# Attention, recurrence and experts on one core: the first stage split into two halves of the heads, all of it ahead of the tiles

## What is computed

```python
# 1. cross attention of every position to one target per element, 16 heads of 8
q = shard(query @ Wq + bq).reshape(b, H * s, hd)     # H = 16, s = 128, hd = 8
scores = softmax(einsum('bnd,bdh->bnh', q, k) / sqrt(hd))
context = einsum('bnh,bhd->bnd', scores, v)
context = context.transpose(0, 2, 1).reshape(b, s, H * hd)   # row of the result: d * 16 + h
# 2. linear attention: softmax of q over 8 values, elu(k) + 1, cumulative sums over the heads, @ Wo, + x
# 3. a gated recurrence over the 128 positions, then a top-2 of 8 experts FFN of its states, + x
```

## Time and profile before

| what | value |
|---|---|
| median of 3 runs | 395.06 us (394.81 to 395.1) |
| the profiled execution | 397.36 us, its span 395.7 us |
| PE busy | 369.5 us (93%) |
| VectorE busy | 336.7 us (85%) |
| ScalarE busy | 273.5 us (69%) |
| GpSimd busy | 264.3 us (67%) |
| mean granted TensorE clock | 0.939 |

### The profile page before, as it was taken

The page is one execution under the profiler, slowest core; times in us unless marked ns, Lnnn a source line. Parts: engine busy times, 40 slices in busy tenths (PEclk is TensorE's granted clock), DMA queues, the critical chain, the costliest instruction groups (busy, mean ns, idle before and its releaser), DMA issues.

```text
span 395.7 us, 9033 instructions
## 1 busy us (share of the span) xinstructions
PE 369.5 (93%) x2404; PEld 302.6 (76%) x2404; DVE 336.7 (85%) x1226; ACT 273.5 (69%) x1040; POOL 264.3 (67%) x293
## 2 busy tenths in 40 slices
PE   4999985578999999999999999999999999999995
PEld 2688851366788888888888888888888888878874
DVE  2677756876599999999999999999999999998640
ACT  2455545234488888888888887788788888877663
POOL 3977607883567777777777777777777777786000
PEclk9999995555599999999999999999999999999999
DMA  6600000000000000000000000000000000000000
GB/s 173 241 2 0 3 0 0 2 0 1 0 9 7 8 10 7 9 8 9 10 12 9 7 9 7 8 10 7 9 8 9 8 8 8 7 11 12 9 8 13
DMA packets 7584, 6.74 MB, mean 17 GB/s; under 512 B 880, under 2 KB 6256, under 8 KB 7536
## 3 DMA queue, kind: packets, MB, share of 16 engines
q1 hardware_dynamic: 7536, 6.19, 5.2%
HBM read 4.09 MB, written 2.10 MB: 16 GB/s over the span
## 4 chain that ended last, share of the span: by engine, by line
DVE 50%; issue 14%; PE 13%; ACT 1%; POOL 1%; DVEq 1%
DVE kvs L939 13%; PE bank L372 12%; DVE att L948 7%; DVE mem L997 5%; DVE h L1017 4%; DVE rden L931 4%; DVE bank L1002 3%; DVE bank L1009 3%; DVE kvs L917 3%; DVE bank L899 2%; PE bank L514 1%; DVE bank L923 1%; DVE bank L971 1%; POOL qc L329 1%; DVE res L988 1%
## 5 line engine op out<-in xcount | busy, mean ns | idle before, releaser
L329 POOL TENSOR_TENSOR qc<-kvs,qn 128x512 f32<-128x512 f32 x64 | 81.4, 1272 | 19.5 <-DVE kvs L939 15.2
L372 PEld LDWEIGHTS bank<-h,gwh 128*128 128x128 f32 x512 | 72.7, 201 | 20.8 <-DVE h L1017 17.9
L317 POOL TENSOR_TENSOR kv<-kv,qkv 128x512 f32<-128x512 f32 x64 | 81.0, 1268 | 3.3 <-DVE kvs L939 0.8
L939 DVE TENSOR_TENSOR_SCAN kvs<-bank,kv 128x256 f32<-128x256 f32 x128 | 81.4, 659 | 0.5 <-POOL qc L329 0.5
L372 PE MATMUL bank<-h,gwh 128*128 128x32 f32 x512 | 76.5, 274 | 4.7 <-DVE h L1017 4.6
L709 ACT ACTIVATE hid<-bank,gw 128x128 f32<-128x128 f32 x256 | 76.3, 372 | 1.6 <-PE bank L372 1.5
L372 PE MATMUL bank<-w,h 128*128 128x512 f32 x128 | 73.0, 653 | 0.0
L372 PE MATMUL bank<-w,hsq 128*128 128x128 f32 x512 | 71.2, 282 | 1.8 <-ACT hsq L717 1.8
L735 ACT ACTIVATE gt<-bank 128x64 f32<-128x64 f32 x128 | 30.2, 236 | 50.9 <-PE bank L372 49.9
L372 PEld LDWEIGHTS bank<-w,hsq 128*128 128x128 f32 x512 | 62.2, 191 | 3.4 <-ACT hsq L717 2.9
L372 PE MATMUL bank<-h,whw 128*128 128x64 f32 x256 | 52.6, 289 | 0.0
(11 more groups left out here) (112 smaller groups left out, 704.6 us busy)
## 6 DMA issues: line engine op xcount, KB each, us to landing
XT<-in_x_t_dram SPq DMA_DIRECT2D x8, 256.0 KB, 5.6
out_dram<-res SPq DMA_DIRECT2D x32, 64.0 KB
w<-in_w_dram SPq DMA_DIRECT2D x2, 512.0 KB, 5.1
aw<-in_aw_dram SPq DMA_DIRECT2D x1, 192.0 KB, 5.5
gwx<-in_gw_dram SPq DMA_DIRECT2D x1, 128.0 KB, 4.6
gwh<-in_gw_dram SPq DMA_DIRECT2D x1, 128.0 KB, 4.2
cwk<-in_cwk_dram SPq DMA_DIRECT2D x1, 64.0 KB, 1.9
cwv<-in_cwv_dram SPq DMA_DIRECT2D x1, 64.0 KB, 2.0
```

The costliest lines, as they stand in the source:

```text
L317: pool.tensor_tensor(kv[:, a * D:b * D, :].rearrange("p (d e) h -> p d e h", d=D // 2), kv[:, D * D + a:D * D + b, :].unsqueeze(2).broadca ...
L329: pool.tensor_tensor(qc[:, a:b, :, :], kvs[:, a * D:b * D, :].rearrange("p (d e) h -> p d e h", d=D // 2), qn[:, p, a:b, :].unsqueeze(2).b ...
L372: return pe.matmul(dst, w, rhs, start=start, stop=True, skip_group_check=True)
L939: dve.tensor_tensor_scan(flat(kvs[:, a:b, :]), scan_mask, flat(kv[:, a:b, :]), 0.0, ALU.mult, ALU.add).then_inc(kv_sum, 1)
```

## The change

Part 1 is still 16 units, but a unit is now four elements with eight heads. Units 0 to 7 are heads 0 to 7 of all 32 elements, units 8 to 15 heads 8 to 15. A unit's scores fill one bank as before, as four matmuls of 128 columns in place of two of 256; its context is the same four matmuls of 72 columns. All queries are kept (`qT` of 8 groups), and all keys (`kbd` of 32 elements), so GpSimd no longer waits for `s_ps` of an earlier unit. `q_of` for all groups now stands in the first eight units. The two matmuls for `awc` and `qkvb` move from units 12 and 14 to units 5 and 6. The three priming matmuls are gone, since Z, MEM and QKV are now scores banks themselves.

Units 8 to 15 have one bank (`OUT`) for their contexts. `context(u)` there waits for `normalise(u - 1)`, where before it waited for `normalise(u - 2)`.

The ramp of each engine begins with units 9 to 15, and the tiles' part of the ramp is rewritten: on VectorE `add_dims(0)` and `residual(0)` come directly behind `sum_heads(0, 3)`, and all of tile 1, then all of tile 2 come behind them. On PE `qkv_of(2)` and `(3)` go behind `gates_x(0, 0)`. The memsets and small copies that stood behind the last unit stand between units 6 and 7.

```diff
-PAIRS = B // 2
+QUADS = B // GROUP
+HALF = H // 2
...
-        qT = sb("qT", [P, 2, GROUP * P])
-        kbd = sb("kbd", [P, 4, H, H])
+        qT = sb("qT", [P, QUADS, GROUP * P])
+        kbd = sb("kbd", [P, B, H, H])
...
+        def scores_bank(u):
+            return Z if u % 2 else QKV if u < QUADS else MEM
+        def probs_bank(u):
+            return TR if u % 2 else MEM if u < QUADS else HID
+        def context_bank(u):
+            return OUT if u >= QUADS else ATT if u % 2 else DV
...
             def scores(u):
-                pe.wait_ge(q_sb, u // 2 + 1)
+                half, g = u // QUADS, u % QUADS
+                pe.wait_ge(q_sb, g + 1)
                 if u == 0:
-                    pe.wait_ge(kbd0_ok, 2)
-                else:
-                    pe.wait_ge(kbd_ok, 2 * u)
+                    pe.wait_ge(kbd0_ok, 1)
+                pe.wait_ge(kbd_ok, u + 1)
                 at_least(pe, s_sub, u - 1)
...
             def context(u):
                 pe.wait_ge(pT_sb, u + 1)
-                at_least(pe, c_sb, u - 1)
-                pe.wait_ge(vbd_ok, u + 1)
+                at_least(pe, c_sb, u if u >= QUADS else u - 1)
+                pe.wait_ge(vbd_ok, u % QUADS + 1)
...
-            for u in range(PAIRS):
-                if u + 1 < PAIRS:
-                    scores(u + 1)
-                if u % 2 == 0 and u // 2 + 1 < B // GROUP:
-                    q_of(u // 2 + 1)
+            q_of(1)
+            for u in range(QUADS):
+                scores(u + 1)
+                if u + 2 < QUADS:
+                    q_of(u + 2)
                 probs_T(u)
                 if u:
                     context(u - 1)
-                if u == PAIRS - 4:
+                if u == QUADS - 3:
                     pe.wait_ge(w_late, LATE_ALL)
-                    mm(bank[6][:, 0:3 * P], cwoT[:, :], aw[:, :]).then_inc(awc_ps, 1)
-                if u == PAIRS - 2:
+                    mm(HID[:, 0:3 * P], cwoT[:, :], aw[:, :]).then_inc(awc_ps, 1)
+                if u == QUADS - 2:
                     pe.wait_ge(awc_sb, 1)
-                    mm(bank[6][:, 0:3 * P], bco.broadcast_to([P, P]), aw[:, :]).then_inc(awc_ps, 1)
-            pe.wait_ge(s_sub, PAIRS - 1)
-            mm(Z[:, :], w1[:, 0, :], w1[:, 0:4, :].rearrange("p e d -> p (e d)")).then_inc(prime_z, 1)
-            pe.wait_ge(pT_sb, PAIRS - 1)
-            mm(MEM[:, :], w1[:, 0, :], w1[:, 0:4, :].rearrange("p e d -> p (e d)")).then_inc(prime_m, 1)
-            pe.wait_ge(c_sb, PAIRS - 1)
-            mm(QKV[:, :], w1[:, 0, :], w1[:, 0:4, :].rearrange("p e d -> p (e d)")).then_inc(prime_q, 1)
-            context(PAIRS - 1)
+                    mm(HID[:, 0:3 * P], bco.broadcast_to([P, P]), aw[:, :]).then_inc(awc_ps, 1)
+            context(QUADS - 1)
             pe.wait_ge(consts, 2)
-            pe.wait_ge(c_sb, PAIRS)
...
             def ramp():
+                scores(9)
+                probs_T(8)
...
                 qkv_of(0)
                 qkv_of(1)
-                qkv_of(2)
-                qkv_of(3)
                 att_T(0)
                 project_out(0)
                 gates_x(0, 0)
+                qkv_of(2)
+                qkv_of(3)
```

## The result

| | before | the change |
|---|---|---|
| median | 395.08 us (394.81 to 398.7, 4 runs) | 411.26 us (409.25 to 413.11, 4 runs) |
| ratio to before | | 1.0386, 95% interval 1.0307 to 1.0466 |
| profiled execution, its span | 397.36 us, 395.7 us | 413.11 us, 411.4 us |
| mean granted clock in it | 0.939 | 0.921 |

The change is slower by 16.2 us in the medians and by 15.7 us in the spans of the two profiled executions. The forecast was slower by 10.6, 405.6 with a range to 410.0. The direction and the largest term were right; the sum was too small by 5.7 us in the median and by 5.1 in the span.

What follows compares the result with a forecast made beforehand. PE limits the first stage, a VectorE, ScalarE and GpSimd chain the ramp. +3.0 us to `head_max(0)` and +6.8 in the ramp make +9.8; with +0.8 for the clock, 395.06 becomes 405.6 us, range 399.5 to 410.

Steps and rivals of the forecast that it cites:

- The tiles' order in the ramp, +6.8: Ramp, `head_max(0)` to `memory(0, 0, 0)`: tile 1, then tile 2 begin later, making 24.2 us against 17.4.
- PE's walk through the units, 38.7 from `scores(1)` to `context(11)`: First stage: walking the engines' lists from `scores(1)` near 13.9 us puts `context(11)` at 52.6.
- The single bank, 2.12 a context: Last contexts: the one bank spaces them, four times 2.12 us from `context(11)` at 52.6 to `context(15)` at 61.1.
- The clock in this chain: "I take +0.8": Late contexts: low clock likely falls before or at `qkv_of(0)`, +0.8 us, plus 0.85 per context behind the fall.
- +2.5 as the upper end: Late contexts: the most the low clock was taken to cost if it falls before several contexts, up to +2.5 us.
- The start: "`scores(1)` starts near 13.9": Start of PE: `scores(1)` waits for the late keys, near 12.4 us, and starts near 13.9, where it was 12.16.
- The clock in the tiles: unchanged: First three tiles: clock returns in the third tile again, so `memory(0, 0, 0)` to the fourth tile stays about 38 us.
- the likeliest case: Whole kernel: the forecast with the clock returning in the third tile again, 403.5 to 408 us, chance 0.56.
- The rival (one tile sooner): First tiles: the full clock is back one tile sooner, giving 399.5 to 402 us; chance 0.2.

Runs made afterwards that it cites:

- the old order: The changed kernel with tiles 0, 1 and 2 interleaved in the ramp as before on PE, ScalarE and VectorE: 404.08 us, ratio to before 1.0144.
- two banks: The changed kernel with contexts 8 to 15 alternating between banks ATT and OUT, each waiting for normalise(u - 2): 402.21 us, ratio to before 1.0117.
- The fillers: The changed kernel with one extra, never-read matmul of 512 or 384 columns in each gap between contexts 11 to 15: 405.55 us, ratio to before 1.0217.
- the one with the early matmuls: The changed kernel with nine small, never-read identity matmuls in PE's idle time before the first scores: 410.07 us, ratio to before 1.0295.
- two filled versions: The kernel before with never-read matmuls in PE's idle time of ramp and tile 0; the second adds more, also in tile 1: 394.04 and 393.33 us.

## Why the prediction was right and where it was wrong

- **The tiles' order in the ramp, +6.8.** Measured +6.94, and 17.40 with the old order. Every part of the chain came as worked out: tile 1 begins 11.9 behind the first `head_max`, tile 2 6.0 behind that, and GpSimd's `weigh(1)` ends it.
- **PE's walk through the units, 38.7 from `scores(1)` to `context(11)`.** Measured 38.86. The halved scores matmuls cost next to nothing, as taken (a unit with a projection 3.08 us, before 3.06). The match to 0.2 is in part luck: from `scores(1)` to the end of `context(7)` it was 25.6 against 24.9, and the second half won 0.5 of that back.
- **The single bank, 2.12 a context.** Mechanism right, and shown: with two banks it is 4.46 us from the first of the five contexts to the last. Spacing at full clock was 2.2, which adds 0.3 over the four.
- **The clock in this chain: "I take +0.8".** This is the step that was sized wrong. The clock fell inside context 13, and not at `qkv_of(0)`. From `context(11)` to `head_max(0)` it took 10.19 + 4.11 = 14.3 us, where I had 8.5 + 2.5 + 0.8 = 11.8. The fillers gave 2.9 back, and this is what the clock cost, 2.1 more than the term; the other 0.4 is that the bank's turn and the way behind the last context were a little longer at full clock too. I had worked out +2.5 as the upper end and then taken the lower value, because the trace of before had no stretch so sparse. The old-order kernel and the one with the early matmuls have the same chain, and both lost the clock in it as well (context 14 took 1.95 us in each), so the high end was the one to take.
- **The start: "`scores(1)` starts near 13.9".** It started at 16.10, the second term that was sized wrong. I took PE to be at full clock there, since the clock row said 1.00. The durations say otherwise, and those of before would have warned: its first projection took 2.08 us. Most of the 2.2 us is no part of the change. With the same start, the kernel with two banks had `scores(1)` at 14.22, with the durations of full clock: 0.3 above the forecast. The other 1.9 are the half clock. The start of before was caught in both ways too, 12.16 in its own profile and 13.85 and 14.23 in its two filled versions. Like with like, the change starts about 2 us later, and the forecast said 1.7. Which of the two an execution gets was not found, so that the profile of the change had the long durations and that of before the short ones is chance, as far as the runs tell. So about 1.9 of the 15.7 us between the two profiled executions is not the change's; the medians can't be divided like this.
- **The clock in the tiles: unchanged.** 38.34 against 38.04, so the likeliest case held. The rival (one tile sooner) did not happen in this profile, but the first three tiles took 34.1 to 35.1 us in four of the experiments, which is near what it says. What decides which of the two comes was not found.

The sum by measured terms: +3.94 to `scores(1)`, +4.69 from there to the first `head_max` (53.16 against 48.47), +6.94 in the ramp, +0.30 in the first three tiles and -0.17 in the rest make 15.7 us, as the spans do. Against the forecast of 10.6 the start is 2.2 over and the contexts' chain with its clock 2.5; these two are nearly all of the 5.1 that was missed.

## What to carry to other kernels

When a stage is split so that a part of it can start sooner, the order has to use that in the same change; if the second half still stands ahead of everything, only the costs of the split are left. When a rewritten order moves one tile's result forward, count what used to run in the wait for it. And where a change makes TensorE's work as sparse as in this chain, give the low clock its full price in the sum (here 2.9 us), and try one matmul in each gap. Last, compare starts by the durations of the first matmuls before a difference of 2 us is put down to a change.

## What the hardware showed that I had not expected

- The clock fell in a chain of eight 72-column matmuls at a time with gaps of about 1.1 us between them (0.88 in 59 to 60, 0.50 from 60 on); the same chain with a matmul of 384 or 512 columns in each gap kept 1.00.
- In the kernel before the granted clock is shown as 1.00 from the first microsecond, but the first projection took 2.08 us and later ones 1.02.
- The same kernel's executions differ by up to 6 us (394.05 to 400.26 for the kernel before) and the mean granted clock goes with it only in part (394.05 to 396.95 at 0.947).
- Matmuls whose results nobody reads took 2.9 us off the contexts' chain, and 8.6 us off the first three tiles of the kernel before. Where they stood behind the fall of the clock (2.99 us for two), they delayed the next context by 2.1 us.
